# Local attention in pairs of units, four units' lag, and the end of the stage and the front of the recurrence in another order

## The reference, cut to what matters

```
x = x + local(_gn(x))              # group norm, groups of 4 channels
  local: roll by (-3, -3); qkv = x @ w_qkv
         per window and head: softmax(q k^T * 32**-0.5 + bias + mask) v
         out @ w_out + b_out; roll back
t = tokens of x
t = t + linear(_ln(t))             # q, k = elu(.) + 1; cumulative sums of k v^T and k
t = t + ffn(_ln(t))                # Wx with batch norm, then y = sigmoid(Wx_t + y V^T), step by step
```

## Time and profile before

| | |
|---|---|
| runs, us | 1857.97, 1854.97, 1857.34; median 1857.34 |
| profiled execution, us | 1857.33 |
| its span, us | 1855.5 |
| busy in the span | PE 98%, DVE 82%, ACT 66%, POOL 54% |
| mean granted TensorE clock | 0.995 |

### The profile page before, as it was taken

One profiled execution on the slowest core, in us unless ns is written; L12 is line 12 of the kernel. 1 busy time (PEld: TensorE's weight loads), 2 busy tenths in 40 slices (PEclk: granted clock), 3 DMA queues, 4 the chain that ended last, 5 costly groups with the idle time before them and its releaser, 6 DMA issues.

```text
span 1855.5 us, 57715 instructions
## 1 busy us (share of the span) xinstructions
PE 1823.2 (98%) x19600; PEld 1616.4 (87%) x19600; DVE 1523.3 (82%) x4705; ACT 1215.8 (66%) x3180; POOL 1011.1 (54%) x1177
## 2 busy tenths in 40 slices
PE   7999999999999999899999999999999998999998
PEld 6888888888888888799999999999999998888886
DVE  7888888888888888688888888888888887566665
ACT  5877888888888887566666666666666665333333
POOL 6878888888888888533333333333333434432321
PEclk9999999999999999999999999999999999999999
DMA  5333334333333332122222222222223222556543
GB/s 170 104 100 107 106 106 106 107 106 105 104 106 104 103 83 79 46 70 69 69 67 68 70 67 67 70 65 70 66 69 93 67 70 83 210 178 221 188 166 126
DMA packets 207109, 187.02 MB, mean 101 GB/s; under 512 B 14577, under 2 KB 190945, under 8 KB 206817
## 3 DMA queue, kind: packets, MB, share of 16 engines
q1 hardware_dynamic: 205664, 182.14, 33.1%
q10 hardware_dynamic: 1152, 1.13, 0.2%
HBM read 105.95 MB, written 77.27 MB: 99 GB/s over the span
## 4 chain that ended last, share of the span: by engine, by line
PE 54%; issue 27%; POOL 16%; DVE 1%; DMA 1%; POOLq 0%; ACT 0%; ACTq 0%; DVEq 0%; SPq 0%
POOL la_rstd L983 11%; PE k_psum L343 7%; PE k_psum L293 6%; PE k_psum L286 6%; PE k_psum L311 6%; PE k_psum L327 5%; PE k_psum L359 5%; PE k_psum L1393 5%; PE k_psum L1384 5%; PE k_psum L277 4%; POOL la_spread L977 3%; PE k_psum L1374 2%; PE k_psum L1401 2%; POOL la_tn L988 2%; POOLq L39 0%
## 5 line engine op out<-in xcount | busy, mean ns | idle before, releaser
L977 POOL TENSOR_SCALAR la_spread<-la_mv 128x4 f32<-128x4 f32 (+1 forms) x203 | 46.2, 227 | 483.2 <-DVE la_mv L1083 483.1
L606 POOL TENSOR_TENSOR wa_prob<-wa_prob,wa_peak 128x784 f32<-128x784 f32 x128 | 194.8, 1522 | 115.3 <-DVE wa_peak L477 115.3
L924 ACT ACTIVATE la_ve<-k_psum 128x256 f32<-128x256 f32 x196 | 75.6, 385 | 231.9 <-PE k_psum L807 231.9
L983 POOL TENSOR_TENSOR la_rstd<-la_spread,k_exponent 128x4 f32<-128x4 f32 (+1 forms) x203 | 207.7, 1023 | 17.2 <-POOL la_spread L977 0.4
L1458 ACT ACTIVATE sc_y<-k_psum,sc_cols 128x256 f32<-128x256 f32 x207 | 98.2, 474 | 178.6 <-PE k_psum L1393 178.6
L795 PE MATMUL k_psum<-la_uT,la_wt 128*128 128x256 f32 x784 | 202.5, 381 | 0.0
L613 POOL TENSOR_TENSOR wa_prob<-wa_prob,wa_inv 128x784 f32<-128x784 f32 x128 | 195.1, 1524 | 11.3 <-DVE wa_inv L438 11.3
L1039 DVE SCALAR_TENSOR_TENSOR la_fqk<-k_psum,la_raised 128x512 f32<-128x512 f32 x196 | 135.5, 691 | 77.4 <-ACT la_raised L916 77.3
L1184 POOL TENSOR_TENSOR sc_ub<-sc_tb 128x3584 f32<-128x3584 f32 (+6 forms) x22 | 92.9, 4223 | 174.6 <-PE k_psum L1374 173.2
L469 DVE TENSOR_TENSOR wa_prob<-k_psum,wa_bias 128x784 f32<-128x784 f32 x128 | 124.9, 976 | 66.5 <-PE k_psum L311 66.3
L916 ACT ACTIVATE la_raised<-k_psum,la_minus_one 128x512 f32<-128x512 f32 x196 | 134.8, 688 | 44.2 <-PE k_psum L795 44.0
(11 more groups left out here) (134 smaller groups left out, 5298.8 us busy)
## 6 DMA issues: line engine op xcount, KB each, us to landing
t<-la_tn SPq DMA_DIRECT2D x196, 129.0 KB, 2.3
la_xc<-x SPq DMA_DIRECT2D x196, 128.0 KB, 2.1
wa_xT<-in_x_cm SPq DMA_DIRECT2D x124, 196.0 KB, 3.4
sc_tb<-t SPq DMA_DIRECT2D x12, 1806.0 KB, 8.8
out<-sc_ob SPq DMA_DIRECT2D x12, 1792.0 KB, 12.6
wa_xw<-in_x_tok SPq DMA_DIRECT2D x64, 224.0 KB, 2.8
wa_xw<-in_x_tok SPq DMA_DIRECT2D x64, 168.0 KB, 2.4
x<-wa_y SPq DMA_DIRECT2D x64, 168.0 KB, 2.9
```

The lines of the kernel that those rows point to most:

```text
L606: nc.gpsimd.tensor_tensor(s, s, peak[:, k % S, :].unsqueeze(2).broadcast_to([128, PAIRS * HEADS, WIN]), ALU.subtract).then_inc(lowered, 1)
L983: nc.gpsimd.tensor_tensor(rstd[:, n % S, used], spread[:, used], exponent[:, used], ALU.pow).then_inc(rooted, 1)
```

## The change

The local attention's loops go in steps of two units, first = n and second = n + 1. On TensorE the order of the shapes is now: scores of the first, attended values of two units (n-4 and n-3), scores of the second, and then everything that uses the full array. The attended values come four units behind instead of three, and the projection six and five. prob, peak, total, inv and vb have D = 6 slots, qT, kb and pT two. Even units' attended values and projections use bank b_ot, odd ones b_y. ScalarE, VectorE, GpSimd and SP have new orders for a pair. The loads are issued 16 units ahead, and the next stage joins from unit 124 on, on some engines in the middle of the step. In the linear attention the first four units are normalised by another instruction, and half of the last u2 is made on VectorE. At the recurrence's front TensorE gets 3 + 9 products whose results nobody reads, and shift_bn comes behind the copy of fT.

```
-                def step(n, k):
-                    queries(n, k)
-                    turn_probabilities(n - 3, k - 3, 0)
-                    project(n - 4, k - 4)
-                    values(n, k)
-                    group_moments(n, k)
-                    turn_probabilities(n - 3, k - 3, 1)
-                    scores(n, k)
-                    attend(n - 3, k - 3, 0)
-                    attend(n - 3, k - 3, 1)
-                    keys(n + 1, k + 1)
+                def step(n, other):                            # TensorE
+                    first, second = n, n + 1
+                    keys(first, first)
+                    turn_probabilities(n - 4, n - 4, 0)
+                    project(n - 6, n - 6)
+                    queries(first, first)
+                    turn_probabilities(n - 4, n - 4, 1)
+                    values(first, first)
+                    keys(second, second)
+                    turn_probabilities(n - 3, n - 3, 0)
+                    group_moments(n, n)
+                    project(n - 5, n - 5)
+                    queries(second, second)
+                    turn_probabilities(n - 3, n - 3, 1)
+                    values(second, second)
+                    if n >= NU:
+                        other(first)
+                    scores(first, first)
+                    for unit in (n - 4, n - 3):
+                        for h in range(2):
+                            attend(unit, unit, h)
+                    scores(second, second)
+                    if n < NU:
+                        other(first)
+                    other(second)
...
+                def step(n, other):                            # VectorE
+                    aggregate(second, second)
+                    add_bias(n - 1, n - 1)
+                    find_peak(n - 1, n - 1)
+                    residual(n - 6, n - 6)
+                    measure_ahead(n + STATS)
+                    add_up(n - 2, n - 2)
+                    invert(n - 2, n - 2)
+                    if n >= JOIN:
+                        other(first)
+                    group_variance(n, n)
+                    values_out(first, first)
+                    residual(n - 5, n - 5)
+                    add_up(n - 1, n - 1)
+                    invert(n - 1, n - 1)
+                    measure_ahead(n + STATS + 1)
...
+                    add_bias(first, first)
+                    find_peak(first, first)
+                    values_out(second, second)
...
+                def step(n, other):                            # ScalarE
+                    keys_out(first, first)
+                    probabilities_out(n - 4, n - 4, 0)
+                    queries_out(first, first)
+                    probabilities_out(n - 4, n - 4, 1)
+                    exps(n - 2, n - 2)
+                    values_out(first, first)
+                    probabilities_out(n - 3, n - 3, 0)
+                    exps(n - 1, n - 1)
+                    keys_out(second, second)
+                    queries_out(second, second)
+                    probabilities_out(n - 3, n - 3, 1)
+                    values_out(second, second)
+                    if n >= JOIN:
+                        other(first)
+                    attended_out(n - 4, n - 4)
+                    attended_out(n - 3, n - 3)
...
+                def step(n, other):                            # GpSimd
...
+                    lower(n - 1, n - 1)
+                    if n >= JOIN:
+                        other(n)
+                    weigh(n - 2, n - 2)
+                    if n >= FILL:
+                        root(n + 1, n + 1)
+                        normalise(n + 2, n + 2)
+                    keep_tokens(n - 4, n - 4)
+                    if n >= FILL:
+                        normalise(n + 3, n + 3)
+                    keep_tokens(n - 3, n - 3)
+                    weigh(n - 1, n - 1)
+                    lower(n, n)
...
+                        if n < S:
+                            last = nc.vector.scalar_tensor_tensor(u[:, n % S, a, :], xc[:, n % XS, a, :], mv[:, n % S, 0, a, 0:1],
+                                                                  rstd[:, n % S, a:a + 1].broadcast_to([P, C]), ALU.subtract, ALU.mult)
...
         @block.tensor                                         # front of the recurrence
         def _(pe):
+            self.keep_warm(3)
             pe.wait_ge(self.gram_done, 1)
             nc.tensor.matmul(bank[0][:, 0:E], self.cT[:, :], gram[:, :], start=True, stop=True).then_inc(self.pchain, 1)
+            self.keep_warm(9)
             pe.wait_ge(self.chain, counts["scaled"])
```

More of the change, by code:

```diff
@@ L39, in at_least, with pipeline, other @@
         eng.wait_ge(sem, value)
[L42 to L47, removed]
+def pipeline(step, first, last, following, join, prepare):
+    for n in range(first, last, 2):
+        def other(unit):
+            if unit in prepare or unit >= join:
+                next(following)
+        step(n, other)
     for _ in following:
@@ L198, in softmax_view, with attended_bank, projected_bank @@
             return tile[:, k].rearrange("p a b c d -> p (a b c) d")[:, :, 0:WIN]
-        run = dict(first=-AHEAD, last=NU + 6, unroll=XS)
-        JOIN = NU - 3
+        run = dict(first=-AHEAD, last=NU + 8)
+        JOIN = NU - 4
         FILL = 4
+        def attended_bank(n):
+            return b_ot if n % 2 == 0 else b_y
+        def projected_bank(n):
+            return b_y if n >= NU - 2 else attended_bank(n)
         if True:
@@ L244, in await_image @@
                         sp.wait_ge(stored[k], stores_before(NWR * (image + 1), k))
[L246 removed]
+                pipeline(step, **run, following=linear["sync"](sp, await_image), join=JOIN - 3, prepare=(2 - AHEAD, 3 - AHEAD))
             @block.tensor
@@ L431, in add_up @@
                         dve.wait_ge(raised, n + 1)
-                        nc.vector.tensor_reduce(total[:, k % S, :], softmax_view(prob, k % S), AX.X, ALU.add).then_inc(totalled, 1)
+                        nc.vector.tensor_reduce(total[:, k % D, :], softmax_view(prob, k % D), AX.X, ALU.add).then_inc(totalled, 1)
                 def invert(n, k):
@@ L476, in find_peak, with measure_ahead @@
                         dve.wait_ge(biased, n + 1)
[L477 to L482, removed]
-                    residual(n - 4, k - 4)
-                    if not NWR <= n + STATS < STATS:
-                        measure(n + STATS, k + STATS)
-                    group_variance(n, k)
-                    if n == -1:
+                        nc.vector.tensor_reduce(peak[:, k % D, :], softmax_view(prob, k % D), AX.X, ALU.max).then_inc(peaked, 1)
+                def step(n, other):
+                    first, second = n, n + 1
+                    def measure_ahead(unit):
+                        if not NWR <= unit < STATS:
+                            measure(unit, unit)
+                    aggregate(second, second)
[13 more added lines that the diff above has]
+                    measure_ahead(n + STATS + 1)
+                    if n == -2:
                         for later in range(NWR, STATS):
@@ L949, in scale_tokens @@
                     at_least(act, counted, n - S + 1)
-                    for a in range(2):
+                    for a in range(1 if n == UNITS - 1 else 2):
                         last = nc.scalar.activation(u2[:, n % S, a, 0:C], tn[:, n % XS, a, 0:C], ACT.Copy, scale=rstd[:, row, 2 + a:3 + a])
@@ L1165, in load_weights, with keep_warm @@
         sp.dma_start(self.gb[:, 1:2], beta.rearrange("(p a) -> p a", a=1)).then_inc(self.consts, 16)
+    def keep_warm(self, count):
+        for _ in range(count):
+            self.nc.tensor.matmul(self.bank[6][:, 0:C], self.ones[:, :], self.ones[:, :], start=True, stop=True)
     def try_sigmoid(self, act):
```

153 lines of the change are left out of this document (81 added, 72 removed).

## The result

The changed kernel takes 1884.88 us (median of 4 runs, 1883.96 to 1885.78), the kernel before 1856.65 beside it (1854.97 to 1857.97): ratio 1.0152, interval 1.0139 to 1.0164. Forecast were 1852.9, with a range from 1838 to 1868. The loss is 28 us.

What follows compares the result with a forecast made beforehand. The prediction took TensorE's own time to bound the local attention. Its terms, -21.8 + 11.8 + 9.6 + 1 - 3 - 2, summed to -4.4 us, so 1852.9 us from 1857.34, with a range of 1838 to 1868.

Steps and rivals of the forecast that it cites:

- Part 1: Local attention, TensorE: fewer switches between tile shapes save 0.34 us a pair, -21.8 us over 64 pairs.
- Part 2: Even unit's second-half transposes wait 0.19 us for ScalarE's copy of the first half, in 62 pairs: +11.8 us.
- Part 3: Values of the second unit wait 0.64 us for VectorE, delayed by group_variance, in 15 images: +9.6 us.
- Others at nothing: Steady local attention: other buffer guards and waits, including GpSimd's and SP's work, cost no time.
- Part 4: Filling, first two pairs: each second scores waits for add_bias; +1 us, between 0 and 3.
- Part 5: End of local attention: idle and slow-clock time partly gained, with la_u's new form; -3 us, bounds -11 and +3.
- Part 6: Recurrence's front: added matmuls fill TensorE's gap and keep the clock at 2.4 GHz; -2 us, bounds 0 and -3.
- C: Rival: no slack, so values(second) waits for VectorE in each pair; 0.3 us a pair, +19, 1872 us; chance 0.15.
- D: Rival: TensorE's two new shape passages cost together 0.64, so nothing is saved; +22, 1875 us; chance 0.05.

Runs made afterwards that it cites:

- after_ts: Changed kernel with the two 128x1 group-norm instructions (aggregate, group_variance) as tensor_scalar instead of scalar_tensor_tensor: 1854.06 us.
- both edits: Changed kernel with both group-norm instructions as tensor_scalar and, on ScalarE, exps(n-2) moved ahead of queries_out(first): 1846.55 us.
- te_fill: Kernel with both edits, but in the first two pairs TensorE does the first unit's scores straight behind its values: 1846.53 us.
- te_lau: Kernel with both edits, but la_u of the first four linear-attention units back in tensor_scalar: 1847.83 us.
- before_ts: Kernel before the change, with its two 128x1 group-norm instructions as tensor_scalar: 1856.29 us, ratio 0.9999.
- te_cold: Kernel with both edits, without the 3 + 9 matmuls that keep TensorE busy at the recurrence's front: 1849.00 us.
- before_front: Kernel before the change, with only the 3 + 9 matmuls at the recurrence's front added: 1857.84 us, ratio 1.0005.
- ts_dose_stt: Changed kernel with group norm as tensor_scalar, plus an unused 128x1 scalar_tensor_tensor behind aggregate in 56 pairs: 1886.65 us.
- ts_dose_ts: Changed kernel with group norm as tensor_scalar, plus an unused 128x1 tensor_scalar behind aggregate in 56 pairs: 1853.91 us.

## Why the prediction was wrong, step by step

The sum forecast -4.4 us and the time rose by 28. Two of its steps failed for one reason: it took the price of VectorE's group-norm instructions from the place where they stood, and did not ask what holds them at the new one.

**Part 1, switches: right.** Scores cost 0.82 us behind either neighbour and keys 0.86 behind scores (435.27 in the chain). With part 2 the plain pair came out at 11.43 for 11.50. (The 46.9 us that the prediction gives for an image should be 46.81 by its own terms.)

**Part 2: right in place, 0.10 us for 0.19.** It is there in the plain pairs as the 0.49 for 0.39 above.

**Part 3: the step that failed.** The chain was right: with unheld instructions (after_ts) the pair of group_variance waits 11.93 - 11.43 - 0.17 = 0.33 us. The prediction's own formula gives 0.39 if VectorE's three instructions take the 0.63 that they do there, for the 0.88 of the earlier trace rows. Its term took the 0.88 from a place in which the second one was already held and lasted 0.55, and carried it to another place as if it were its own length. There it lasts 1.55; with that the formula gives 1.64, and 13.21 - 11.43 - 0.17 = 1.61 were measured, for the 0.64 of the forecast. 15 x 0.97 = 15 us of the miss.

**"Others at nothing": the second failure, the same cause.** Of aggregate, which now stands at the head of VectorE's pair, the prediction says nothing at all; 0.34 us in the row of before became 1.74, and 12.17 - 11.43 = 0.74 of it reached TensorE. The first such pair meets no instruction of GpSimd and pays nothing, the last pays little; 13 pairs pay in full, 10 us in all. GpSimd was asked only whether it would be late itself, not whom it stops.

**Part 4: mis-sized.** The scores of unit 4 start 5.6 us later than before, where +1 less two pairs' gain, 0.3, was forecast. With both edits, so free of the holds, they still start 4.7 later. TensorE's order is 1.3 of that, as te_fill shows; for the rest the waits point at VectorE's work on two units in a row. At unit 20, which the sum had at nothing, the changed kernel lost 2.6; with both edits it loses nothing.

**Part 5: the reason was wrong, and no gain is shown.** The 2.45 us were not the form's: in the changed kernel's trace the new form takes 2.49, with GpSimd's weigh and keep_tokens beside it:

```profile
777.70 2.49 DVE L1104 SCALAR_TENSOR_TENSOR la_u<-la_xc,la_mv,la_rstd 128x128 f32<-128x128 f32 x2
```

-1.5 us were measured for -3, and te_lau says that it was not the form. before_ts, whose edit does nothing at the stage's end, takes 49.48 us for this passage too, for the 50.91 of the kernel before and the 49.45 of the changed one. The passage follows the granted clock of the single execution. From unit 120 to the same product the kernel before takes 91.79 us at a mean clock of 0.96 and te_cold 91.87 at 0.96; before_ts takes 90.36 at 0.98 and the changed kernel 90.97 at 0.98. So at an equal clock no gain shows (before_front, at 0.96 too, has 91.09, so traces scatter by some 0.7), and that -1.5 lies near -3 is luck.

**Part 6: right in its mechanism.** -2.0 by the trace, for -2; 1.7 by te_cold's. That it fell on -2.0 is in part luck, since the passage varies with the clock: the means of the four traces without and the ten with the matmuls are 21.7 and 20.4 us, 1.3 apart.

Together: 15 + 10 for the two instructions, 5 for the filling, 2.6 for unit 20, 1.5 for the end and 1 for the last pairs, less 4 for 58 pairs that were 0.07 better than forecast, make 31 of the 31.1 us between forecast and trace (a span 26.7 longer for -4.4). Of the rivals C came nearest, a wait for VectorE in values(second); but it blamed a slack that is too small in each pair, and the plain pairs never wait there. The sign that the prediction set for C or D, an image over 48 us, was there (48.25), with another cause. Its bound for group_variance, 0.88 x 15, was no bound, since it took the row's duration for the instruction's greatest.

## What to carry to other kernels

Before an instruction is moved, look at the spread of its duration over all its records (here 210 to 953 ns for one number a partition): where it spreads, it may be held by something, and then its price belongs to the place, not to the instruction. List what each neighbour engine runs at the new place, and count an instruction like this one, with two tensor inputs in SBUF, until the end of GpSimd's. A form that is not held (here tensor_scalar on one column) costs two changed instructions and was worth 31 us.

## What the runs showed of the hardware that was not expected

- A scalar_tensor_tensor of 128x1 takes 0.21 us alone and up to 2.22 us beside GpSimd's 1.53 us instructions: when two of these follow each other closely, it waits for the rest of the first and for all of the second (ts_dose_stt: it runs from 411.46 to 413.66 us, GpSimd's from 410.64 to 412.17 and from 412.12 to 413.65). tensor_scalar of 128x1 with scalars from SBUF takes 0.26 to 0.28 in all records and is never held; 41 of the 56 in ts_dose_ts lie wholly inside one of GpSimd's long instructions.
- The same operation is held at larger shapes: tensor_scalar of 128x128 took 2.45 us for two (0.34 each is usual), and one of 128x256, in VectorE's preparation of the linear attention, 2.13:

```profile
137.68 2.13 DVE L1091 TENSOR_SCALAR la_bias<-la_bias 128x256 f32<-128x256 f32 x1
...
138.14 1.53 POOL L666 TENSOR_TENSOR wa_prob<-wa_prob,wa_peak 128x784 f32<-128x784 f32 x1
```

(changed kernel with the edit after_ts, timeline; both end within 0.15 us of each other.)
- Time outside the span is not the same for every kernel: 4.1 to 4.6 us in all executions of one, 1.6 to 2.3 in the others, enough to hide a gain of 2 us that the trace shows.
